# A gated cross-attention block with a seven-product FFN: the opening re-ordered, the first chunk's middle layer done plainly, and the weight sums moved from GpSimd to VectorE

## The reference, cut to what matters

```python
# x: (2, 2048, 512) float32; ctx: (2, 128, 512); 16 heads of 32
q = layernorm(x) @ Wq + bq
k, v = ctx @ Wk + bk, ctx @ Wv + bv                    # 128 keys per batch
a = softmax(q @ k.T / sqrt(32)) @ v                    # per head
x = x + tanh(g_xattn[0]) * (a @ Wo + bo)
h = concat([layernorm(x), -layernorm(x)])              # 1024 features
h = relu(s0 * h @ sign(k0)) * 2                        # k0: 1024 x 2048 booleans, weight +1 or -1
h = relu(s1 * h @ sign(k1)) * 2                        # k1: 2048 x 2048
x = x + tanh(g_ffn[0]) * (s2 * h @ sign(k2))           # k2: 2048 x 512
```

## Time and profile before

| | |
|---|---|
| median of the three runs | 1627.11 us |
| profiled execution, whole / its span | 1626.49 / 1624.5 us |
| TensorE busy | 1533.9 us, 94% of the span |
| VectorE busy | 959.6 us, 59% |
| ScalarE busy | 679.9 us, 42% |
| GpSimd busy | 231.1 us, 14% |
| DMA traffic | 121.04 MB, mean 75 GB/s |

### The profile page before, as it was taken

The page is one execution under the profiler, slowest core; times in us unless marked ns, Lnnn a source line. Parts: engine busy times, 40 slices in busy tenths (PEclk is TensorE's granted clock), DMA queues, the critical chain, the costliest instruction groups (busy, mean ns, idle before and its releaser), DMA issues.

```text
span 1624.5 us, 47490 instructions
## 1 busy us (share of the span) xinstructions
PE 1533.9 (94%) x20208; PEld 1308.2 (81%) x20208; DVE 959.6 (59%) x1942; ACT 679.9 (42%) x1584; POOL 231.1 (14%) x287
## 2 busy tenths in 40 slices
...
PEclk8777899999999999999999999999999999999999
...
GB/s 281 58 66 36 47 60 98 61 85 76 51 97 53 103 66 85 67 60 92 54 99 60 92 67 82 77 52 95 56 100 66 82 73 59 95 52 99 34 28 15
DMA packets 278233, 121.04 MB, mean 75 GB/s; under 512 B 243465, under 2 KB 259849, under 8 KB 277897
## 3 DMA queue, kind: packets, MB, share of 16 engines
...
...
## 4 chain that ended last, share of the span: by engine, by line
PE 87%; DVE 8%; ACT 2%; issue 1%; DMA 1%; SPq 0%; POOL 0%; DVEq 0%; ACTq 0%
PE bank L1161 24%; PE bank L1162 24%; PE bank L1177 7%; PE bank L1178 7%; PE bank L1125 6%; PE bank L1126 6%; PE bank L1065 2%; PE bank L1049 2%; PE bank L1066 2%; PE bank L1067 2%; PE bank L1050 2%; PE bank L1051 2%; PE bank L1093 1%; DVE H L819 1%; PE bank L1058 1%
## 5 line engine op out<-in xcount | busy, mean ns | idle before, releaser
L1161 PE MATMUL bank<-H,W 128*128 128x128 f16 x7168 | 836.7, 220 | 31.8 <-ACT C L616 14.5
L1162 PE MATMUL bank<-H,W 128*128 128x128 f16 x7168 | 837.0, 220 | 0.0
L1161 PEld LDWEIGHTS bank<-H,W 128*128 128x128 fp8e5 x7168 | 702.5, 98 | 45.0 <-issue 37.5
L1162 PEld LDWEIGHTS bank<-H,W 128*128 128x128 fp8e5 x7168 | 704.1, 98 | 7.5
L1125 PE MATMUL bank<-hT,W 128*128 128x256 f16 x1024 | 229.7, 275 | 3.7 <-ACT Fp L633 2.1
L1126 PE MATMUL bank<-hT,W 128*128 128x256 f16 x1024 | 229.7, 275 | 0.0
L529 ACT ACTIVATE Pf<-bank,nmax 128x128 f32<-128x128 f32 x512 | 145.9, 368 | 164.4 <-DVE nmax L785 162.7
L477 POOL TENSOR_TENSOR attn<-pvs 128x128 f32<-128x128 f32 x120 | 76.1, 634 | 946.6 <-DVE pvs L798 946.6
L1177 PE MATMUL bank<-W,h 128*128 128x512 fp8e5 x512 | 194.0, 379 | 1.6 <-DVE h L831 1.6
L1178 PE MATMUL bank<-W,h 128*128 128x512 fp8e5 x512 | 194.0, 379 | 0.0
L823 DVE TENSOR_TENSOR C<-bank,C 128x256 f32<-128x256 f32 x192 | 81.2, 423 | 172.2 <-ACT C L616 95.0
...
## 6 DMA issues: line engine op xcount, KB each, us to landing
Qst<-q_bounce SPq DMA_DIRECT2D x120, 128.0 KB, 2.8
...
q_bounce<-Qhl SPq DMA_DIRECT2D x120, 64.0 KB
...
PT<-Phl SPq DMA_TRANSPOSE x120, 3.1
...
```

The costliest lines, as they stand in the source:

```text
L1161: mm(o, w, H0[:, 0, i, b_of, :], start=first, stop=False, skip_group_check=True)
L1162: last = mm(o, w, H0[:, 1, i, b_of, :], start=False, stop=i == PAIRS - 1, skip_group_check=True)
```

## The change

1. **Opening.** A key item K now makes one quarter of the features for one batch (eight items of 128 columns, not four of 256). The first four come at once, before Wq is cut; the other four (the second batch) come late, at units 4 to 7. The scalars are computed after Wq's cuts. Score items S run one ahead of their exponents (new item EX). W0 is built on VectorE alone (one shift and two shift-and-combine instructions per quarter, on 32-bit words). The second V item comes last: on TensorE between WO and T2, on VectorE and ScalarE behind T2.
2. **Chunk 1's first layernorm** (LN, N1, T1) leaves the opening and goes behind slots 0 and 1 of chunk 0's FFN; all other woven items of chunk 0 come three slots later (`WEAVE_0`, `LATER`).
3. **Chunk 0's middle layer** is done plainly: per group 128 matmuls of 256 columns in seven slots (`PLAIN`), no sums of activations, two results of 512 columns each straight from the banks.
4. **W1's sums** are all made on VectorE (`LATE_WEIGHTS`), fifteen during chunk 0's FFN and one at slot 9 of chunk 1. GpSimd makes none.
5. Some `wait_apart` on TensorE (a wait and a nop) become plain waits.

```diff
+    PLAIN = [(0, (0, 1)), (0, (2, 3)), (0, (4, 5)), (0, (6, 7)), (1, (0, 1, 2)), (1, (3, 4, 5)), (1, (6, 7))]
+    PLAIN_ENDS = (3, 6)
...
+    LATER = 3
+    WEAVE_0 = {slot + LATER: items for slot, items in WEAVE.items()}
+    for kind in ("LN", "N1", "T1"):
+        for t in range(TT):
+            WEAVE_0.setdefault(0 if kind == "LN" else t, []).append((1, (kind, t)))
...
-        ("CX", 0), ("CX", 1), ("LN", 0), ("LN", 1), ("N1", 0), ("N1", 1), ("K", 0), ("T1", 0), ("T1", 1), ("KM", 0),
-        ("SCALARS", 0), ("CUT_Q", 0), ("CUT_Q", 1), ("CUT_Q", 2), ("CUT_Q", 3), ("XB", 0), ("XB", 1),
-        ("Q", 0), ("K", 1), ("KM", 1))]
-    BETWEEN = {0: [("Q", 1)], 1: [("V", 0)], 2: [("K", 2), ("KM", 2), ("CUT_O", 0)], 3: [("Q", 2), ("CUT_O", 1)],
-               4: [("K", 3), ("KM", 3), ("CUT_O", 2)], 5: [("Q", 3), ("CUT_O", 3)], 6: [("V", 1), ("K0", 0), ("W0", 0)],
-               7: [("W0", 1)], 8: [("W0", 2)]}
+        ("CX", 0), ("CX", 1), ("LN", 0), ("LN", 1), ("N1", 0), ("N1", 1), ("K", 0), ("T1", 0), ("T1", 1), ("K", 1),
+        ("K", 2), ("K", 3), ("KM", 0), ("CUT_Q", 0), ("CUT_Q", 1), ("CUT_Q", 2), ("CUT_Q", 3), ("SCALARS", 0),
+        ("KM", 1), ("Q", 0), ("KM", 2), ("V", 0), ("S", 0), ("Q", 1), ("KM", 3))]
+    BETWEEN = {1: [("XB", 0), ("XB", 1)], 2: [("Q", 2)], 4: [("K", 4), ("Q", 3)], 5: [("K", 5), ("CUT_O", 0)],
+               6: [("K", 6), ("CUT_O", 1), ("W0", 0)], 7: [("K", 7), ("CUT_O", 2), ("W0", 1)],
+               8: [("CUT_O", 3), ("W0", 2)], 9: [("W0", 3)]}
     for k in range(U + 2):
-        FIRST += [(0, ("S", k))] if k < U else []
+        FIRST += [(0, (kind, k + ahead)) for kind, ahead in (("S", 1), ("EX", 0), ("PV", -2)) if 0 <= k + ahead < U]
         FIRST += [(0, item) for item in BETWEEN.get(k, ())]
-        FIRST += [(0, (kind, k - behind)) for kind, behind in (("PT", 1), ("PV", 2)) if 0 <= k - behind < U]
+        FIRST += [(0, ("PT", k - 1))] if 0 <= k - 1 < U else []
     FIRST += [(0, ("CT", 0)), (0, ("CT", 1))]
-    FIRST += [(1, (kind, t)) for kind in ("LN", "N1", "T1") for t in range(TT)]
-    FIRST += [(0, item) for item in (("WO", 0), ("WO", 1), ("N2", 0), ("T2", 0), ("N2", 1), ("T2", 1), ("W0", 3))]
+    FIRST += [(0, item) for item in (("WO", 0), ("WO", 1), ("N2", 0), ("N2", 1))]
+    LAST_V = [(0, ("V", 1))]
+    FIRST_PE = FIRST + LAST_V + [(0, ("T2", 0)), (0, ("T2", 1))]
+    FIRST += [(0, ("T2", 0)), (0, ("T2", 1))] + LAST_V
...
+    LATE_WEIGHTS = ({0: (0, 0), 2: (0, 1), 4: (1, 0), 6: (0, 2), 8: (0, 3), 10: (2, 0), 11: (1, 1), 13: (1, 2),
+                     15: (1, 3), 17: (0, 4), 18: (3, 0), 19: (2, 1), 21: (2, 2), 23: (2, 3), 27: (1, 4),
+                     29: (3, 1), 31: (3, 2), 33: (3, 3), 36: (2, 4)}, {9: (3, 4)})
...
+            def weight_step(q, step):
+                Wg, made = W1[:, q], w1_made[q]
+                L11, L12, L21, L22 = (Wg[:, b] for b in range(4))
...
+                if step == 1:
+                    dve.wait_ge(w1_signs, q + 1)
+                    V_.tensor_tensor(Wg[:, A_S3], L11, L21, ALU.subtract, saturate=False).then_inc(made, 1)
...
+            def plain_product(q, s):
+                half, pairs = PLAIN[s]
...
+                if s in (0, 4) and q > 0:
+                    pe.wait_ge(h1_lo, 4 * (q - 1) + 2 * half + 2)
+                for i in pairs:
+                    if q == 0:
+                        pe.wait_ge(l0_lo, i + 1)
+                    for j in range(2):
+                        o = banks[half][:, j * CHUNK:(j + 1) * CHUNK]
+                        for b in range(2):
+                            w = W1[:, q, 2 * half + b, i, j * P:(j + 1) * P]
+                            mm(o, w, H0[:, 0, i, 2 * b:2 * b + 2, :], start=i == j == b == 0, stop=False,
+                               skip_group_check=True)
+                            last = mm(o, w, H0[:, 1, i, 2 * b:2 * b + 2, :], start=False,
+                                      stop=i == PAIRS - 1 and b == 1, skip_group_check=True)
+                last.then_inc(l1_done, 1)
...
+                    if n < 2 and f == 1:
+                        pe.wait_ge(h1_lo, nth(0, NH, NH - 1))
```

277 lines of the change are left out of this document (148 added, 129 removed).

## The result

The changed kernel takes 1605.9 us (median of four, 1603.5 to 1607.6) against 1627.5 for the kernel before in the same comparison: a ratio of 0.987, interval 0.985 to 0.989. That is 1.3% faster, inside the 2% that was called no change. The forecast was 1598, its range 1580 to 1612.

The account below looks back on a forecast made before the run. TensorE bounds steady chunks, so all gain lies before chunk 1: 87.6 + 15 + 95.3 + 1.5 + 8 = 207.4 us for its start against 236.1, 28.7 less, giving 1598 us, range 1580 to 1612.

Parts of the forecast that it names:

- The opening to CT: Opening up to the transposes CT: CT starts at 71.5 us, 13.8 earlier than before.
- The 28.2 for S(0): Opening: first score item starts at about 28.2 us, against 30.76 before, with K1 to K3 now ahead of Wq's cuts.
- the rule on the two engines: VectorE with two SBUF inputs and GpSimd reading SBUF exclude each other; chunk 0's adds 2 to 3 us more, not summed.
- The loop's length: Opening, S(0) to CT: 43.3 us for the rounds, against 54.5 before, with S(k+1) ahead of EX(k).
- CT to L0: End of the opening, CT to chunk 0's first layer: 16.1 us against 19.9, so L0 starts at 87.6.
- What V(1) releases: Chunk 0's start: late V(1) delays the keys' store, ScalarE's first copy and Q(0); cost +15 us, bounds 0 and 18.
- The floor: TensorE's least time for chunk 0, with the plain middle layer: 95.3 us, plus 1.5 at the boundary to chunk 1.
- VectorE's lag: Chunk 0: fifteen weight sums and chunk 1's normalisation on VectorE delay PV and WO; +8 us, bounds 2 and 16.
- The rest: Plain waits and chunk 1's one weight sum cost or gain nothing; the waits under 0.3 us a chunk.
- The keys' store binds: Start of chunk 0: rival said the keys' store does not bind, its term falls away; 1586 us, chance 20%.
- VectorE's gaps are not enough: Chunk 0 and opening: rival said VectorE has gaps enough, lag 2 us and loop 4 less; 1588 us, chance 13%.
- it would have been slower: Chunk 0: rival, VectorE's float8 sums cost up to 5.73 us each; 1643 us, slower from about 4.4, chance 3%.

Follow-up runs that it names:

- masks later: Changed kernel, GpSimd's masked copies of keys 1 to 3 held until Q(0)'s low part is made: 1605.85 us.
- W0 on GpSimd: Changed kernel, W0's quarters made as before the change, two shifts on VectorE and four subtracts on GpSimd: 1609.5 us.
- Keys first: Changed kernel, sync queue issues the keys' store and reload before the wait for V(1) and the third k1 load: 1593.2 us.
- V(1) early: Changed kernel, V's second item back between the opening's units of attention, sync queue as changed: 1596.5 us.
- sums spread: Kernel with Keys first, seven of chunk 0's fifteen weight sums moved to chunk 1, the others mostly away from attention's slots: 1597.0 us.
- normalisation back: Changed kernel, chunk 1's LN, N1 and T1 back in the opening behind CT, chunk 0's weave three slots earlier: 1604.9 us.
- load last: Kernel with Keys first and normalisation back, third k1 load put behind chunk 1's T1 transposes on the sync queue: 1581.7 us.

## Why the prediction was right in the sum, and where its steps failed

**1. The opening to CT.** Forecast 71.5, measured 74.6: S(0) 5.2 us later than put, the loop 41.2 us instead of 43.3. The 28.2 for S(0) left out two things that the change itself brings. GpSimd's copies for K1 to K3 run beside Wq's cuts and the scalars; masks later gave 2.6 of the 5.2 us back in its profile. And V(0) now stands ahead of S(0) on TensorE, 4.7 us long, where it stood behind it: from Q(0)'s start to S(0) it takes 7.4 us where it took 5.1, and with the masks later V(0) alone holds S(0), 3.3 us beyond Q(0)'s low part. The prediction weighed the rule on the two engines only for GpSimd's adds in chunk 0, not here, where it had its first effect. The Trainium skill, page "SBUF — State Buffer", section "SBUF: two separate sides", calls the shared port pair an exclusive lock that is held for the whole instruction. The traces here agree for instructions with both operands in SBUF: 0.69 to 4.3 us with W0 on GpSimd, 2.49 to 0.35 for the mask instructions when the adds of X no longer stand beside them.

The loop's length was near, its reason wrong. The prediction laid it on S(k+1) ahead of EX(k), and that is worth nothing. Of the 13.3 us by which the loop shrank, V(1)'s absence gives 4.3 and W0's move off GpSimd 6.3. The remaining 2.7 were not tested. V(0), 3.6 us within the loop before, has left it too, which is no gain: S(0) comes 2.7 us later than before. Besides, before, S stood twice behind a Q item,

```profile
48.66 0.59 PE L1032 MATMUL bank<-h,Qhl 128*128 128x512 f16 x1 [4.02 <-DVE Qhl L781]
...
61.31 0.58 PE L1032 MATMUL bank<-h,Qhl 128*128 128x512 f16 x1 [3.83 <-DVE Qhl L781]
```

where in the new order no S waits over 1.1 us. Either would be enough; which it is stays open.

**2. CT to L0.** 17.0 against 16.1. The reason given, that chunk 1's LN no longer stands in VectorE's queue, fell: with it back, L0 was no later.

**3. What V(1) releases.** The mechanism was right in each link: first copy, sync queue, transposes, Q(0). k_kept came 18.4 us after V(1), 17.5 were taken; Q(0) began 26.4 us after L0, forecast 23.6. The cost was sized at 15, bound 18, and is 10.9 + 4.1 + 4.8 = 19.8, outside its bound: the clock's share, which only the bound mentioned, is a term of its own. This is the larger part of what chunk 0 missed by (125.2 against 119.8). Keys first and V(1) early, two ways to free the same queue, gave 12.7 and 9.4 us of it.

**4. The floor.** 95.3 and 1.5: measured 95.4 and 1.6.

**5. VectorE's lag.** Forecast 8, measured 7.8. The sums spread shows that without the sums it is gone; but with the weave three slots earlier and the normalisation out of chunk 0, the same fifteen sums leave 2.6. So it is the sums where the change puts the attention items, and not the sums alone. Its stops are mostly where the step put them: 3.7 us at PV(1) to PV(4), forecast 4.8, and all four ended by the exponents of the next unit, as the step said of the banks; 1.4 at PV(5) and PV(7), forecast none; 2.7 at WO(0), forecast 2.8. The rule that was weighed here and left out of the sum is borne out for just the two adds that it was applied to, those of PV(6) and PV(7). GpSimd's last two attention adds ahead of CT take 2.43 us, the six before them 0.45, and beside each of the two stands a sum on VectorE:

```profile
184.86 2.43 POOL L469 TENSOR_TENSOR attn<-pvs 128x128 f32<-128x128 f32 x1 [4.90 <-DVE pvs L807]
...
189.69 2.43 POOL L469 TENSOR_TENSOR attn<-pvs 128x128 f32<-128x128 f32 x1 [1.18 <-DVE pvs L807]
```

```profile
184.69 2.28 DVE L964 SCALAR_TENSOR_TENSOR W<-W 128x2048 fp8e5<-128x2048 fp8e5 x1
...
189.53 2.28 DVE L968 TENSOR_TENSOR W<-W 128x2048 fp8e5<-128x2048 fp8e5 x1
```

The first of them is in the chain that ends the stop of 2.7 us at WO(0): ScalarE's part of xs, and so the DMA transposes, follow it. The step had 2.8 there for another reason, so that size is partly luck; with the normalisation back, where the last two adds take 0.45 and 0.46, the stop is 0.4.

**6. The rest.** Plain waits: 93.6 against 92.7 for chunk 1, later chunks as before.

**The rivals.** The keys' store binds: it takes 9.7 us from issue to landing with the sync queue otherwise empty (64.09 to 73.83 with the load last) and 10.6 in the change, so it never is quick. VectorE's gaps are not enough. A float8 sum is 2.28 us in both forms, far from the 4.4 from which it would have been slower.

So chunk 1 starts 9.4 us later than forecast (216.8 against 207.4): S(0) gives 5.2 of it, CT to L0 0.9 and chunk 0 5.4, nearly all of that step 3, less 2.1 for the loop. The medians are 7.9 us apart, and the range was wide enough above the forecast to hold that. The late keys' term was right in kind and too small; the loop's near hit was luck. And one part of the change, chunk 1's normalisation moved into chunk 0 with the weave three slots later, brings nothing: with the late keys in front of it it is free, with the keys early it costs 6 us.
